# Four GNN layers on one core: layers 1 and 2 scale a tile in one operation and add it in another, and all engines get new orders of work

## What is computed

```python
# layer 0: 8 heads of 32, q = k = v, then an MLP
n = layer_norm(h, gamma1, beta1); qkv = n.reshape(.., 8, 32)
s = qkv @ qkv.T / sqrt(32);  out = softmax(where(adj > 0, s, -inf)) @ qkv
h = h + out;  x = x + h + gelu(layer_norm(h, gamma2, beta2) @ W1 + b1) @ W2 + b2
# layers 1 and 2: 4 heads of 64, graph attention
g = h @ W;  e = leaky_relu(src[i] + dst[j], 0.2);  x = x + softmax(where(adj > 0, e, -big)) @ g
# layer 3: 4 heads of 64, q, k, v and Wo
x = x + relu(softmax(where(adj | eye, q @ k.T / 8, -big)) @ v @ Wo + bo)
```

## Time and profile before

| | |
|---|---|
| median of 3 runs | 4377.15 us (4377.02 to 4380.96) |
| the profiled execution's own time | 4382.13 us |
| its span, first to last instruction | 4380.3 us |
| TensorE busy, share of the span | 4104.0 us, 94% |
| TensorE weight loads (beside the matmuls) | 1923.7 us, 44% |
| VectorE | 3246.0 us, 74% |
| ScalarE | 2163.2 us, 49% |
| GpSimd | 417.4 us, 10% |
| chain that ended last | PE 57%, DVE 30%, ACT 5%, SPq 3% |

### The profile page before, as it was taken

One profiled execution on the slowest core, in us unless ns is written; L12 is line 12 of the kernel. 1 busy time (PEld: TensorE's weight loads), 2 busy tenths in 40 slices (PEclk: granted clock), 3 DMA queues, 4 the chain that ended last, 5 costly groups with the idle time before them and its releaser, 6 DMA issues.

```text
span 4380.3 us, 59537 instructions
## 1 busy us (share of the span) xinstructions
PE 4104.0 (94%) x22884; PEld 1923.7 (44%) x22884; DVE 3246.0 (74%) x6985; ACT 2163.2 (49%) x3361; POOL 417.4 (10%) x469
## 2 busy tenths in 40 slices
...
DMA packets 212314, 193.92 MB, mean 44 GB/s; under 512 B 144448, under 2 KB 179008, under 8 KB 203584
## 3 DMA queue, kind: packets, MB, share of 16 engines
...
...
## 4 chain that ended last, share of the span: by engine, by line
PE 57%; DVE 30%; ACT 5%; SPq 3%; DMA 2%; issue 2%; POOL 1%; DVEq 0%; ACTq 0%; POOLq 0%
PE M L422 10%; PE M L435 9%; DVE PG L1017 6%; DVE PP L903 6%; PE M L488 5%; PE M L446 4%; DVE x L934 4%; PE O L474 4%; PE S L355 4%; PE O L537 4%; DVE Q L913 4%; DVE PP L1046 3%; PE M L579 3%; PE O L368 2%; SPq L1181 2%
## 5 line engine op out<-in xcount | busy, mean ns | idle before, releaser
L1017 DVE SCALAR_TENSOR_TENSOR PG<-g,tcg,mT 128x512 f32<-128x512 f32 x1024 | 694.3, 743 | 36.0 <-PE O L478 17.0
L622 ACT ACTIVATE PP<-S,reach 128x1024 f32<-128x1024 f32 x512 | 542.4, 1110 | 238.6 <-PE S L355 189.2
L903 DVE TENSOR_TENSOR PP<-PP,mT 128x1024 f32<-128x1024 f32 x512 | 597.7, 1214 | 32.0 <-ACT PP L622 32.0
L474 PE MATMUL O<-PG,V 128*32 128x512 f32 x4096 | 536.5, 643 | 10.7 <-DVE PG L1017 9.3
L647 ACT ACTIVATE z<-x,nb,rs 128x256 f32<-128x256 f32 x384 | 209.2, 597 | 540.1 <-DVE nb L893 540.1
L422 PE MATMUL M<-hT,W 128*128 128x512 f32 x1024 | 456.0, 598 | 5.1 <-ACT hT L657 2.0
L435 PE MATMUL M<-W,H 128*128 128x256 f32 x2048 | 459.7, 378 | 0.0
L1128 POOL TENSOR_SCALAR ve<-mv 128x4 f32<-128x4 f32 x192 | 111.3, 580 | 3409.3 <-DVE mv L861 3409.3
L979 DVE TENSOR_TENSOR x<-x,M 128x256 f32<-128x256 f32 x128 | 52.6, 411 | 490.5 <-PE M L435 490.4
L435 PEld LDWEIGHTS M<-W,H 128*128 128x128 f32 x2048 | 377.3, 189 | 71.6 <-issue 10.6
L355 PE MATMUL S<-hT 32*128 32x512 f32 x2048 | 325.6, 707 | 56.3 <-ACT PP L622 28.4
...
## 6 DMA issues: line engine op xcount, KB each, us to landing
...
mT<-z SPq DMA_TRANSPOSE x128, 3.7
m<-V SPq DMA_TRANSPOSE x128, 2.5
```

The costliest lines, as they stand in the source:

```text
L474: e.matmul(k.O[0][r:r + 32, :], s.V[:, jt, 64 * hh + 32 * v:64 * hh + 32 * v + 32], p[:, u, :], start=(jt == 0), stop=(jt == NT - 1))
L622: e.activation(p[:, 2 * pair:2 * pair + 2, :], k.S[:, 2 * pair:2 * pair + 2, :], ACT.Exp, bias=k.reach[:, 7:8], scale=SC0).then_inc(k.e0.s ...
L903: e.tensor_tensor(p[:, 2 * pair:2 * pair + 2, :], p[:, 2 * pair:2 * pair + 2, :], s.mT[:, jt:jt + 1, :].to_broadcast([128, 2, N]), ALU.mul ...
L1017: e.scalar_tensor_tensor(out=p[:, u, :], in0=s.T[hh], scalar=s.tcg[:, 1, hh, jt:jt + 1], in1=s.mT[:, jt, :], op0=ALU.max, op1=ALU.mult).th ...
```

## The change

Five things are done to the kernel.

1. In layers 1 and 2, `b2r` on VectorE is one multiplication of a whole tile, from `M` into `V`, as in layer 0, and `fin` adds `V` to `x` in a second operation. The bank is free after the first (`take` waits for `nrm`), and the sums `bst` of the next layer norm still wait for the second.
2. The orders of TensorE, ScalarE, VectorE, GpSimd and SyncE are new. On TensorE `qt(b1, 1)` stands right behind `qt(b1, 0)`, ahead of `sc0(b1, 0)`; the transposes `tt(b3, 3, ..)` of layer 3 come before `sc0(b1, 2)`; `pv3` and `vp` move by a place or two; `rd3` stands behind `tt(b2, 1, ..)`. On VectorE `gw(b2, 1, 0)` stands behind all four tiles of `b2r(b3, 2, ..)` and three of the `fin`, where it stood ahead of the last tile's `b2r`.
3. `masks(b0, 0)` moves from ahead of `wo(b4, ..)` to behind `pa0(b1, 3)`, near the end of the iteration; `ln0(b0, 0)` is now in the same iteration, on ScalarE between `sc3(b3, 1)` and `sc3(b3, 2)`. `ln1` moves ahead of and among the `pj` of layer 1, and `zb(b1)` with it.
4. `diag` is done an iteration earlier, a few steps behind `masks(b1, 1)`, whose DMA transposes it must await. SyncE issues the transposes of `m3` before the load of the next adjacency and before `trow` and `tbc` of layer 2.
5. Semaphores: `diag` and `zb` signal within VectorE only, and `lw` and `lt` are shared by layers 1 and 2 (`nth` gives the landing of each). This adds and removes no instruction of an engine's work.

The diff, cut; the orders that are not shown are reordered in the same manner.

```diff
@@ -66,6 +66,9 @@
     def at(self, b):
         return self.sems[b % self.n], 16 * self.per * (b // self.n + 1)
 
+    def nth(self, b, i):
+        return self.sems[b % self.n], 16 * (self.per * (b // self.n) + i + 1)
+
...
@@ -384,7 +387,7 @@
     def b2r(self, b, L, t):
         e, k, s = self.e, self.k, self.k.of(b)
         M = k.M[t % 2]
-        self.take(f"M{t % 2}", k.add[L].at(b, t) if L else k.nrm.at(b, t))
+        self.take(f"M{t % 2}", k.nrm[L].at(b, t))
         if L == 0:
...
@@ -928,32 +931,26 @@
         e, k, s = self.e, self.k, self.k.of(b)
         M = k.M[t % 2]
         self.marked("inverse", L, b, t)
-        if L:
-            for h in range(4):
-                x = s.x[:, t, 64 * h:64 * h + 64]
-                r = e.scalar_tensor_tensor(out=x, in0=M[:, 64 * h:64 * h + 64], scalar=s.ri[:, t, h:h + 1], in1=x,
-                                           op0=ALU.mult, op1=ALU.add)
-            r.then_inc(k.add[L].sem, 1)
-        else:
-            e.tensor_tensor(s.V[:, t, :].rearrange("p (h d) -> p h d", d=32),
-                            M[:, 0:256].rearrange("p (h d) -> p h d", d=32),
-                            s.ri[:, t, 0:8, None].to_broadcast([128, 8, 32]), ALU.mult).then_inc(k.nrm.sem, 1)
+        n = 4 if L else 8
+        e.tensor_tensor(s.V[:, t, :].rearrange("p (h d) -> p h d", h=n), M[:, 0:256].rearrange("p (h d) -> p h d", h=n),
+                        s.ri[:, t, 0:n, None].to_broadcast([128, n, D // n]), ALU.mult).then_inc(k.nrm[L].sem, 1)
 
     @step
     def fin(self, b, L, t):
         e, k, s = self.e, self.k, self.k.of(b)
-        if L == 0:
...
     def fin(self, b, L, t):
         e, k, s = self.e, self.k, self.k.of(b)
-        if L == 0:
-            self.wait_ge(*k.zb.at(b, 0))
-            self.wait_ge(*k.nrm.at(b, t))
-            e.tensor_tensor(s.z[:, t, :], s.z[:, t, :], s.V[:, t, :], ALU.add).then_inc(k.add[0].sem, 1)
+        if L == 0 and t == 0:
+            self.marked("bias", 0, b, 0)
+        self.wait_ge(*k.nrm[L].at(b, t))
+        dst = s.x if L else s.z
+        e.tensor_tensor(dst[:, t, :], dst[:, t, :], s.V[:, t, :], ALU.add).then_inc(k.add[L].sem, 1)
...
@@ -1265,10 +1255,10 @@
         do.w2(b2, 3)
         do.den3(b4)
         do.gpv(b3, 2, 0)
-        do.rd3(b4)
         do.gpv(b3, 2, 1)
         do.tt(b2, 1, 0)
         do.tt(b2, 1, 1)
+        do.rd3(b4)
         do.pj(b2, 1, 0)
         do.pj(b2, 1, 1)
...
@@ -1283,213 +1273,211 @@
         do.b2r(b3, 2, 2)
         do.b2r(b3, 2, 3)
         do.qt(b1, 0)
+        do.qt(b1, 1)
         do.sc0(b1, 0)
         do.gpv(b2, 1, 0)
         do.gpv(b2, 1, 1)
         do.sc0(b1, 1)
         do.gpv(b2, 1, 2)
         do.gpv(b2, 1, 3)
-        do.qt(b1, 1)
-        do.pv0(b1, 0)
+        do.tt(b3, 3, 0)
+        do.tt(b3, 3, 1)
+        do.sc0(b1, 2)
         do.b2r(b2, 1, 0)
         do.b2r(b2, 1, 1)
-        do.sc0(b1, 2)
+        do.pv0(b1, 0)
+        do.pv0(b1, 1)
         do.dn0(b1, 0)
         do.b2r(b2, 1, 2)
         do.b2r(b2, 1, 3)
-        do.pv0(b1, 1)
-        do.tt(b3, 3, 0)
-        do.tt(b3, 3, 1)
         do.sc0(b1, 3)
+        do.pv0(b1, 2)
...
         do.gmax(b3, 2)
+        do.pa3(b4, 2)
         do.gprep(b3, 2)
-        do.pa3(b4, 2)
         do.pa3(b4, 3)
         do.masks(b1, 1)
+        do.resid0(b2)
+        do.bst(b1, 1, 0)
+        do.bst(b1, 1, 1)
+        do.diag(b1)
+        do.bag(b1, 1, 0)
+        do.bag(b1, 1, 1)
         do.gvals(b3, 2)
...
         do.gw(b3, 2, 0)
-        do.w2(b2, 1)
+        do.gw(b3, 2, 1)
         do.bst(b2, 3, 1)
-        do.bst(b1, 1, 2)
         do.w2(b2, 2)
...
         do.pj(b2, 1, 0)
         do.pj(b2, 1, 1)
         do.pj(b2, 1, 2)
+        do.zb(b1)
         do.pj(b2, 1, 3)
         do.gmax(b2, 1)
+        do.gprep(b2, 1)
         do.rb3(b4)
-        do.gprep(b2, 1)
         do.gvals(b2, 1)
-        do.masks(b0, 0)
         do.wo(b4, 0)
         do.wo(b4, 1)
         do.rc(b3, 2, 0)
@@ -1498,98 +1486,116 @@
         do.b2r(b3, 2, 1)
         do.rc(b3, 2, 2)
         do.b2r(b3, 2, 2)
+        do.fin(b3, 2, 0)
+        do.rc(b3, 2, 3)
+        do.b2r(b3, 2, 3)
         do.bst(b3, 5, 0)
+        do.fin(b3, 2, 1)
+        do.fin(b3, 2, 2)
         do.bst(b3, 5, 1)
+        do.gw(b2, 1, 0)
+        do.bst(b3, 5, 2)
+        do.gw(b2, 1, 1)
+        do.fin(b3, 2, 3)
...
         do.sc0(b1, 0)
-        do.nb(b3, 5)
         do.sc0(b1, 1)
         do.pa0(b1, 0)
         do.rc(b2, 1, 0)
         do.rc(b2, 1, 1)
         do.b2r(b2, 1, 0)
         do.b2r(b2, 1, 1)
+        do.fin(b2, 1, 0)
+        do.sc0(b1, 2)
+        do.rc(b2, 1, 2)
+        do.b2r(b2, 1, 2)
+        do.rc(b2, 1, 3)
         do.bst(b2, 4, 0)
-        do.rc(b2, 1, 2)
-        do.bst(b2, 4, 1)
-        do.rc(b2, 1, 3)
-        do.b2r(b2, 1, 2)
+        do.fin(b2, 1, 1)
         do.b2r(b2, 1, 3)
-        do.sc0(b1, 2)
...
 def sync_program(do):
 
-    for it in range(0, NB + 5):
-        b0, b1, b2, b3, b4, b5 = it, it - 1, it - 2, it - 3, it - 4, it - 5
+    for it in range(1, NB + 6):
+        b1, b2, b3, b4, b5, b6 = it - 1, it - 2, it - 3, it - 4, it - 5, it - 6
+        do.store(b6)
+        do.load(b2)
+        do.masks_t(b2, 0)
         do.masks_t(b2, 1)
+        do.loada(b1)
+        do.trow(b4, 2)
+        do.tbc(b4, 2)
+        do.rrow(b5)
         do.rbc(b5)
         do.trow(b3, 1)
         do.tbc(b3, 1)
-        do.store(b5)
-        do.load(b1)
-        do.masks_t(b1, 0)
-        do.trow(b3, 2)
-        do.loada(b0)
-        do.tbc(b3, 2)
-        do.rrow(b4)
     do.end()
```

More of the change, by code:

```diff
@@ L207, in signal @@
             return {i: Signal(sem(f"s_{name}_{i}"), per[0]) for i in range(per[1], per[2])}
[L209 to L215, removed]
+        (self.mk, self.nb, self.m0, self.qa, self.qa3, self.add, self.nrm, self.w2a, self.xx, self.pjs, self.gmx,
+         self.gex, self.gv, self.gm, self.mx3, self.sh3, self.m3, self.r3, self.o3, self.woa, self.stat, self.z0,
+         self.v0, self.sqa, self.qtc, self.e0, self.oc0, self.od0, self.y0, self.zr, self.hv, self.gelu, self.pjc,
+         self.gtc, self.spc, self.goc, self.god, self.qka, self.vva, self.e3, self.oc3, self.od3, self.rdc,
+         self.qt, self.sc0, self.pv0, self.dn0, self.b2r, self.tt, self.w1, self.w2, self.pj, self.srt, self.gpv,
+         self.qk, self.vp, self.sqm, self.sc3, self.pv3, self.dn3, self.den3, self.rd3, self.wo, self.rs,
+         self.parg) = [signal(name) for name in SIGNALS]
     def of(self, b):
@@ L1041, in sc3 @@
         p = k.P[jp]
-        self.wait_ge(*k.diag.at(b, 0))
+        if c == 0:
+            self.marked("diag", 0, b, 0)
         for ju in range(2):
@@ L1306, in tensor_program @@
         do.sc0(b1, 4)
-        do.pv0(b1, 2)
         do.pv0(b1, 3)
@@ L1312, in tensor_program @@
         do.qk(b3, 3)
+        do.vp(b3, 0)
         do.sc0(b1, 6)
+        do.pv0(b1, 4)
         do.sq3(b3, 0)
[L1315 removed]
         do.pv0(b1, 5)
         do.dn0(b1, 2)
+        do.sc0(b1, 7)
         do.sq3(b3, 1)
[L1319 to L1342 removed]
+        do.pv0(b1, 6)
+        do.sc3(b3, 0)
+        do.tt(b2, 2, 0)
+        do.tt(b2, 2, 1)
+        do.pv0(b1, 7)
+        do.vp(b3, 1)
+        do.dn0(b1, 3)
+        do.sc3(b3, 1)
+        do.b2r(b1, 0, 0)
+        do.b2r(b1, 0, 1)
+        do.pv3(b3, 0)
+        do.sc3(b3, 2)
+def scalar_program(do):
+    for it in range(0, NB + 4):
+        b0, b1, b2, b3, b4 = it, it - 1, it - 2, it - 3, it - 4
         do.ln2(b2, 0)
         do.ln2(b2, 1)
[L1345 removed]
         do.pj(b3, 2, 2)
         do.pj(b3, 2, 3)
+        do.ln2(b2, 2)
         do.ln2(b2, 3)
+        do.ln0(b1, 1)
         do.tt(b2, 0, 0)
+        do.ln0(b1, 2)
         do.tt(b2, 0, 1)
```

213 lines of the change are left out of this document (90 added, 123 removed).

## The result

The changed kernel takes 4243.38 us (median; 4241.09 to 4245.99), the kernel before beside it 4377.34: a ratio of 0.9692, 95% interval 0.9676 to 0.9709. The forecast, 4309, had the sign right and half the size; the range began at 4262.

A forecast was written before the change was run, and what follows sets the result against it. The prediction took TensorE, 94% busy, as the bound, its gaps and clock dips as the gain: -1.6 - 0.45 - 2.1 + 1.0 + 0.35 + 0.35 = -2.45 us, x 29 = -71, +3 = -68: 4309 us; range 4262 to 4378.

The forecast's parts named there:

- Split, early `qt` and `gw`: From `wo` through the four `gpv` of layer 1: predicted -1.6 - 2.1 + 1.0 = -2.7 us per iteration.
- The walk: Step through the new order from the end of `wo` to `sc0`: TensorE's waits shrink, -1.6 us per iteration.
- the dips: TensorE's clock falling to half around `sc0` and `gpv`; taken to go once gaps close, -2.1 us per iteration.
- `gw` +1.0: `gw(b2, 1, 0)` starts later on VectorE and then paces TensorE's `gpv`: +1.0 us per iteration.
- Rival C: VectorE, from `rc(b3, 2, 0)` to `pa0(b1, 3)`, takes the gain back: 4380 us, no change; chance 0.11.
- `tt(b3, 3, ..)` and small margins, +0.70: `tt` comes earlier and meets ScalarE's fourth `lnz`, +0.35; margins under 0.1 in four places, +0.35 us per iteration.
- `wo` (-0.45): TensorE's 0.87 wait ahead of `wo` shrinks as `ln1` moves ahead of ScalarE's `grow` copy: -0.45 us per iteration.
- The ends, +3: Start: first graph without cover, +3, and late `ln0`, +2; end: earlier `grow` and shorter tile chains, -2; sum +3 us.
- Rival B: TensorE's clock still falls, as small waits remain, and `gw`'s 1.0 isn't paid: 4341 us; chance 0.21.
- D: Rival: the four `gpv` of layer 1 wait 2.8 us for `gw` and the clock stays low: 4422 us; chance 0.13.
- The signs of being wrong: `ln0(b0, 0)` or `diag` showing up in TensorE's waits, or the row `g` landing late for `gw`.

The follow-up runs named there:

- e4: Kernel before with the split, `qt(b1, 1)` directly behind `qt(b1, 0)`, and the fourth `b2r(b3, 2)` tile ahead of `gw(b2, 1, 0)` on VectorE: 4384.3 us.
- e5: Kernel before with dummy transposes, which nobody reads, in TensorE's gaps behind the `b2r` tiles of layer 2 and `qt(b1, 0)`: 4362.62 us.
- r7: Changed kernel with `bst`, `bag` and `fin` items, together 2.4 us, moved on VectorE from behind `pa0(b1, 1)` to ahead of `sc0(b1, 3)`: 4291.28 us.

## Why the prediction was wrong in size

Forecast were -68 us, measured -134 (136 between the profiled spans). Of the 68 missing ones 51 lie in the 29 iterations, which gained 4.2 and not 2.45 each, and 17 at the ends.

- **Split, early `qt` and `gw`: right.** The walk gave -1.6 and the dips -2.1, `gw` +1.0; measured -2.8 for the three. Apart they are near as well: the idle time goes down by 1.75 in e4 (2.68 to 0.93), the cured clock gives 2.3 there in e5 (24.99 to 22.72), which leaves about +1.2 for `gw`. VectorE paces the `gpv` as said (the first 2.28 for 11 matmuls, waiting 0.23 for L1014), and the tile operation of all three layers is one group, at the 418 ns of the earlier trace rows, with its addition at 411 (groups of VectorE: busy us, mean ns; idle before):

```profile
L935 DVE TENSOR_TENSOR V<-M,ri 128x256 f32<-128x256 f32 x384 | 155.3, 418 | 6.6
...
L945 DVE TENSOR_TENSOR x<-x,V 128x256 f32<-128x256 f32 x256 | 100.0, 411 | 0.0
```

- **That this gain reaches the end: right by luck.** The sum let 2.45 us an iteration go through to the end without asking what else holds TensorE 17 us further on. Rival C named the danger ("VectorE takes it back") and gave it 0.11, but put its price on eight `fin` and its limit on VectorE's work as a whole. The runs show that C happens in full when only the form and `qt` change (e4: no gain), and that what lifts it is the order *across* `pa0(b1, 1)`: it ends 3.1 us earlier in the changed kernel, just as TensorE comes 3.0 earlier. The items that r7 puts back account for 1.7 of the 3.1; the rest was not taken apart. The prediction mentions none of these moves.
- **`tt(b3, 3, ..)` and small margins, +0.70: not incurred.** TensorE shows a wait of 0.36 at `sc0(b1, 3)` and no other there. Measured over that part, up to `sc0(b1, 5)`: -0.2.
- **The rest of the iteration: the step that failed most, 1.2 of the 1.8 us.** I booked `wo` (-0.45) and took all other work behind the scores at its old length, as if all idle time stood between `wo` and the first `sc0`. The trace of the kernel before has 1.84 us of idle time an iteration behind `sc0(b1, 5)`, the wait ahead of `wo` among it. Even `wo` was mis-sized: the 0.87 of the row that I took the earlier trace rows isn't the mean. The waits summed over the span, before and after:

```profile
PE M L576 <- ACT z L694: 17.3, 30, 0.9
```
```profile
PE M L579 <- ACT z L697: 12.6, 29, 0.4
```

That is 0.58 and 0.43, so -0.15. Yet -1.3 was there. About half of it is idle time that the trace shows, 1.84 before and 1.16 after; 0.38 ahead of `sc0(b1, 7)` and 0.15 ahead of a tile of `b2r(b2, 0, ..)` are gone. The other half is busy time, for the same matmuls. By step, from start to start in one iteration: `b2r(b2, 0, ..)` takes 0.4 less, `pj(b3, 2, ..)` 0.2, `gpv` with `rd3` 0.2, `pj(b2, 1, ..)` with its `gpv` 0.1, `dn3` 0.2, `sc3` 0.1, `pv0` 0.4 more. Two groups of the changed kernel (busy, mean ns; idle before):

```profile
L449 PE MATMUL M<-wx,hT 128*128 128x264 f32 x1024 | 255.0, 397 | 3.7 <-DVE V L935 1.6 <-ACT hT L658 1.4 <-DVE stt L982 0.8
L477 PE MATMUL O<-PG,V 128*32 128x512 f32 x4096 | 548.9, 603 | 17.5 <-DVE PG L1014 16.0 <-ACT g L703 1.5
```

Before they had 264.6 busy at 406 ns and 536.5 at 643: the first lost 9.6 us, and the second, which holds the low clock in its old mean, gained 12.4 in all. So the mean of one is no measure of the time that a group holds the engine.

One of the new orders in this part was tried, `tt(b2, 2, ..)` ahead of `pv0(b1, 7)`: taking it back (r6) costs 2.1 us an iteration, all behind `sc0(b1, 5)`, more than the 1.3 that the part gained. The prediction doesn't mention this move. How the 1.3 divides among the orders stays open.
- **The ends, +3: wrong.** The filling iterations gained 9.7 and the draining ones 4.4, like full ones; I priced only what the first graph lacks in cover. That is 17 us, a quarter of the miss.
- **Rival B fell.** The clock is 0.99 or 1.00 in the middle windows. The Trainium skill's section on psum-queue depth-cycling (TensorE: Matmul & The Clock Gate) has small idle spells between banks make the clock fall again and again; with waits of 0.45, 0.19, 0.17 and 0.23 left in a row the changed kernel doesn't show it. Nor does a cured clock mean time: e4 and e5 have 0.987 and 0.989 and gain nothing and 15 us.
- **D fell:** `gw` costs TensorE some 1.2 us by the difference above, 0.23 of it ahead of the first `gpv`, and not 2.8.
- **The signs of being wrong didn't come.** Neither `ln0` (L595) nor `diag` is named in TensorE's waits, and VectorE waits for the row `g` twice in the whole run (11.0 us); ScalarE waits 2.4 an iteration for `mT`, and no wait of TensorE behind that is named.

The Trainium skill, page Perfetto Trace Analysis, section Identifying the Most-Contended Engine, which I had set aside, warns that TensorE's busy share doesn't tell how near it is to its limit. The runs agree in one point: the busy time fell by 58.5 us with the same matmuls. Apart from the 2.1 us of the clock I had taken TensorE's busy time in an iteration for work.
